# Diff attention: projections in three split terms, with their weights split when the stage begins and streamed in afterwards

## The reference

```
def _L1_attn_ref(x, W_attn, W_proj, lambda_q1, lambda_k1, lambda_q2, lambda_k2):
    B, T, E = x.shape                    # 4, 512, 512
    C = E // 2;  H = 16;  hd = E // H // 2;  scale = hd ** (-0.5)
    qkv = x @ W_attn                     # 512 x 1536
    q1, k1, q2, k2 = (qkv[..., n * C:(n + 1) * C].reshape(B, T, H, hd) for n in range(4))
    v = qkv[..., 4 * C:6 * C].reshape(B, T, H, 2 * hd)
    lam = jnp.exp(jnp.dot(lambda_q1, lambda_k1)) - jnp.exp(jnp.dot(lambda_q2, lambda_k2)) + LAMBDA_INIT
    attn1 = jnp.einsum('bthd,bshd->bhts', q1, k1) * scale
    attn2 = jnp.einsum('bthd,bshd->bhts', q2, k2) * scale
    score = jax.nn.softmax(attn1 - lam * attn2, axis=-1)
    out = jnp.einsum('bhts,bshd->bthd', score, v)
    return ((1.0 - LAMBDA_INIT) * out.reshape(B, T, E)) @ W_proj
...
x = x + _L1_attn_ref(_layernorm(x, axis=-1), ...)
```

## Time and profile before

| | us |
|---|---|
| median of 3 runs | 2392.21 (2390.53 to 2397.4) |
| the profiled execution | 2390.07 |
| its span, from the first to the last instruction | 2388.3 |
| PE busy | 2145.8 (90%) |
| DVE busy | 1730.0 (72%) |
| POOL busy | 1047.4 (44%) |
| ACT busy | 944.9 (40%) |

### The profile page before, as it was taken

One profiled execution on the slowest core, in us unless ns is written; L12 is line 12 of the kernel. 1 busy time (PEld: TensorE's weight loads), 2 busy tenths in 40 slices (PEclk: granted clock), 3 DMA queues, 4 the chain that ended last, 5 costly groups with the idle time before them and its releaser, 6 DMA issues. The chain is left out here.

```text
span 2388.3 us, 24939 instructions
## 1 busy us (share of the span) xinstructions
PE 2145.8 (90%) x7344; PEld 1102.4 (46%) x7344; DVE 1730.0 (72%) x2983; ACT 944.9 (40%) x1808; POOL 1047.4 (44%) x798
## 2 busy tenths in 40 slices
PE   4999999999999997897899998999789999999858
PEld 2555455555545552434555555464333434334234
DVE  2887788778788875886888988889455363655554
ACT  1442333334424433664656556465123232332321
POOL 2452453333425511233899898999411011110142
PEclk8999999999999998998999999999889999999879
DMA  7000000000000002466645535362322121221121
GB/s 265 19 23 19 19 18 23 18 22 23 14 23 19 23 23 86 166 232 237 220 149 195 179 109 213 115 222 82 118 76 75 46 75 53 71 71 49 49 110 53
DMA packets 95564, 214.87 MB, mean 90 GB/s; under 512 B 15832, under 2 KB 33112, under 8 KB 93032
## 3 DMA queue, kind: packets, MB, share of 16 engines
q1 hardware_dynamic: 77192, 156.18, 20.1%
q10 hardware_dynamic: 17760, 57.42, 6.7%
q0 software_dynamic: 512, 0.13, 0.0%
HBM read 146.30 MB, written 42.07 MB: 79 GB/s over the span
## 5 line engine op out<-in xcount | busy, mean ns | idle before, releaser
L1532 POOL TENSOR_TENSOR s_state<-s_b_rows,s_delta_u 128x1024 f32<-128x1024 f32 x128 | 303.5, 2386 | 37.0 <-DMA s_b_rows<-scan_bc 34.5
L1576 DVE TENSOR_TENSOR_SCAN s_state<-s_decay,s_state 128x512 f32<-128x512 f32 x256 | 305.0, 1212 | 15.5 <-ACT s_decay L1518 13.2
L834 POOL TENSOR_SCALAR a_prob<-a_prob,a_rsum 128x256 f32<-128x256 f32 x256 | 143.0, 577 | 385.8 <-DVE a_rsum L714 385.7
L1691 PE MATMUL c_bank<-c_xn_parts,c_w_parts 128*128 128x512 f32 (+1 forms) x1056 | 269.3, 405 | 6.5 <-DMA c_w_parts<-ffn_weights_lo 6.5
L1518 ACT ACTIVATE s_decay<-s_delta,s_a 128x512 f32<-128x512 f32 x256 | 173.5, 689 | 225.4 <-DVE s_state L1576 219.6
L384 DVE TENSOR_SCALAR f_picks<-f_mask,f_lut_xor,f_lut 128x260 int32<-128x260 int32 x512 | 225.9, 514 | 8.1 <-DVE f_mask L375 1.1
L1691 PEld LDWEIGHTS c_bank<-c_xn_parts,c_w_parts 128*128 128x128 f32 (+1 forms) x1056 | 195.9, 187 | 66.3 <-issue 20.7
L506 PE MATMUL a_bank<-a_xn_t,a_wq 128*128 128x512 f32 x512 | 224.3, 592 | 0.0
L567 PE MATMUL a_bank<-a_wo,a_out_t 128*128 128x512 f32 x512 | 222.3, 592 | 0.0
L2126 ACT ACTIVATE d_prob_t<-d_score 128x512 f32<-128x512 f32 x256 | 138.9, 595 | 194.5 <-PE d_score L2008 193.5
L394 DVE COPY_PREDICATED f_picks<-f_mask,f_picks 128x260 int32<-128x260 int32 x448 | 192.6, 489 | 20.8
(11 more groups left out here) (210 smaller groups left out, 3626.9 us busy)
## 6 DMA issues: line engine op xcount, KB each, us to landing
s_b_rows<-scan_bc SPq DMA_DIRECT2D x64, 512.0 KB, 3.7
c_w_parts<-ffn_weights_hi ACTq DMA_DIRECT2D x39, 512.0 KB, 3.6
c_w_parts<-ffn_weights_lo ACTq DMA_DIRECT2D x39, 512.0 KB, 4.6
f_idx<-in_idx SPq DMA_DIRECT2D x64, 130.0 KB, 2.1
ffn_weights<-f_picks SPq DMA_DIRECT2D x64, 130.0 KB, 1.8
d_qs<-d_hi SPq DMA_DIRECT2D x128, 64.0 KB, 2.0
d_ks<-d_hi SPq DMA_DIRECT2D x128, 64.0 KB, 2.0
d_factor<-in_factors SPq DMA_DIRECT2D x16, 512.0 KB, 3.6
```

The source lines that it names most:

```text
L1532: pool.tensor_tensor(self.state[:, s], row.broadcast_to([P, 2, T]), self.delta_u[:, h % 2], ALU.mult) \
L1576: dve.tensor_tensor_scan(self.state[:, s, e, :], self.decay[u % 2][:], self.state[:, s, e, :], 0.0, ALU.mult, ALU.add).then_inc(self.scann ...
L1691: mm = nc.tensor.matmul(banks[b][0:width[o], :], w_parts[:, n % SLOTS, w, at:at + width[o]], xn_parts[:, x_, k, :], start=((k, w, x_) == t ...
```

## The change

The q, k and v projections are done in three split terms of F32R instead of one F32 product: weights and normed features are each split into a rounded part and a rest, and a chain has 3 x 4 products (hi x hi, lo x hi, hi x lo).

- Features: ACT now rounds all four feature tiles (`xn_t[:, 0]`), and DVE subtracts to get the rest (`xn_t[:, 1]`); before, each of the two copied two tiles.
- Weights: SP loads them in 12 pieces of 256 KB into the memory of the probabilities. ACT rounds each piece, POOL subtracts to get the rest. The v parts stay in place (`wv`). The eight q and k units (512 KB each with both parts) are stored to a scratch in DRAM, from where SP loads them again for every pass, one unit of q and one of k per group (`load_unit`), into one buffer each.
- `load_unit` for the next group waits until PE has finished the projection that reads the buffer. In SP's order both loads stand ahead of the group's `stack`.
- The norm's tile now lies in the memory of `rsum` and `out_t`. The next sequence's norm is therefore applied in group 1, after `finish`, and no longer in group 0.
- The row of ones in `ks` is set in two steps, since units lie in a part of `ks` (and of `qs`) until they are stored.

```
+            def load_raw(m):
+                kind, n = PIECES[m]
+                if m >= SLOTS:
+                    sp.wait_ge(w_split, m - SLOTS + 1)
...
+                sp.dma_start(raw[:, m % SLOTS, :], source).then_inc(raw_in[m % SLOTS], 16)
+            def store_parts(m):
+                sp.wait_ge(w_split, m + 1)
+                sp.dma_start(scratch["diff_parts"][:, unit_of(*PIECES[m])], parts_of(PIECES[m]).bitcast(F32)) \
+                    .then_inc(w_stored, 16)
+            def load_unit(ring, in_pass, kind, after, g):
+                b, turn = ring.at((kind, after), in_pass)
+                sp.wait_ge(ring.full[b], turn)
+                m = "qk".index(kind)
+                sp.dma_start(unit[:, m].bitcast(F32), scratch["diff_parts"][:, unit_of(kind, g)]) \
+                    .then_inc(unit_in[m], 16)
...
             def one_pass(i, more):
                 for g in range(GROUPS):
                     if more or g + 2 < GROUPS:
-                        stack(ring, i, (g + 2) % GROUPS)
+                        pg = (g + 2) % GROUPS
+                        if more or g + 3 < GROUPS:
+                            for kind in "qk":
+                                load_unit(ring, i, kind, pg, (pg + 1) % GROUPS)
+                        stack(ring, i, pg)
...
             for g in range(2):
                 stack(first, 0, g)
+            for m, piece in enumerate(PIECES):
+                if piece[0] != "v":
+                    store_parts(m)
+            sp.wait_ge(w_stored, 16 * 2 * GROUPS)
+            for kind in "qk":
+                load_unit(first, 0, kind, 1, 2)
             load_factors(0, 0)
...
-            def project(ring, in_pass, kind, g):
+            def project(ring, in_pass, kind, g, parts):
                 b, turn = ring.at((kind, g), in_pass)
                 pe.wait_ge(ring.free[b], turn)
-                lo = "qk".index(kind) * D + g * P
-                for k in range(KD):
-                    mm = nc.tensor.matmul(banks[b][:], w[:, k, lo:lo + P], xn_t[:, k, :],
-                                          start=(k == 0), stop=(k == KD - 1))
+                for n, (wp_, xp) in enumerate(TERMS):
+                    for k in range(KD):
+                        w = parts[:, wp_, k * P:(k + 1) * P]
+                        mm = nc.tensor.matmul(banks[b][:], w, xn_t[:, xp, k, :], start=(n == 0 and k == 0),
+                                              stop=(n == len(TERMS) - 1 and k == KD - 1))
...
                         if st < 2 and proj_on:
-                            project(ring, i, "qk"[st], pg)
+                            pe.wait_ge(unit_in[st], (n + 1) * 16)
+                            project(ring, i, "qk"[st], pg, unit[:, st])
...
                     if g:
                         finish(n - 1, g - 1)
+                    if g == 1 and more:
+                        dve.wait_ge(acc_free, n + 1)
+                        norm_apply(nc, dve, norm, x, i + 1)
```

More of the change, by code:

```diff
@@ L175, with __init__ @@
 class Norm:
[L178 removed]
+    def __init__(self, core, sb, tag, xn=None):
         self.stats_done = core.sem(f"{tag}_ln_stats")
@@ L187, in __init__ @@
         self.rstd = sb(f"{tag}_rstd", [P, TT], F32)
-        self.xn = sb(f"{tag}_xn", [P, TT, D], F32)
+        if xn is None:
+            tile = sb(f"{tag}_xn", [P, TT, D], F32)
+            xn = [tile[:, tt, :] for tt in range(TT)]
+        self.xn = xn
 def start_at_one(eng, *sems):
@@ L242, in norm_ahead @@
     for tt in range(TT):
-        nc.vector.tensor_scalar(norm.xn[:, tt, :], x[:, i, tt, :], ahead.mean_var[:, tt, 0:1],
+        nc.vector.tensor_scalar(norm.xn[tt], x[:, i, tt, :], ahead.mean_var[:, tt, 0:1],
                                 ahead.rstd[:, tt:tt + 1], ALU.subtract, ALU.mult) \
@@ L268, in norm_tensor @@
             mm = nc.tensor.transpose(banks[b][:, tt * P:(tt + 1) * P],
-                                     norm.xn[:, tt, k * P:(k + 1) * P], ident[:])
+                                     norm.xn[tt][:, k * P:(k + 1) * P], ident[:])
         mm.then_inc(ring.full[b], 1)
@@ L1832, in stage_diff_attention @@
     VD = D // DH
-    w = sb("d_w", [P, KD, 3 * D], F32)
+    unit = sb("d_unit", [P, 2, 2, KD * P], F32R)
+    wv = sb("d_wv", [P, 2, KD, D], F32R)
     wp = sb("d_wp", [P, KD, D], F32)
@@ L1838, in stage_diff_attention @@
     coef = sb("d_coef", [P, 1], F32)
-    norm = Norm(core, sb, "d")
-    xn_t = sb("d_xn_t", [P, KD, T], F32)
+    xn_t = sb("d_xn_t", [P, 2, KD, T], F32R)
     hi = sb("d_hi", [P, 2, T], F32R)
@@ L1850, in stage_diff_attention, with parts_of, unit_of @@
     out_t = sb("d_out_t", [P, GROUPS, T], F32)
+    norm = Norm(core, sb, "d", xn=[rsum[:]] + [out_t[:, g, :] for g in range(1, GROUPS)])
+    PARTS_AT = {("q", 0): unit[:, 0], ("k", 0): unit[:, 1]}
+    for n, step in enumerate([("q", 1), ("k", 1), ("q", 2), ("k", 2), ("q", 3), ("k", 3)]):
+        rows, h = (qs, 2 * HG + 2 * n) if n < HG else (ks, 3 * HG + 2 * (n - HG))
+        PARTS_AT[step] = rows[:, h:h + 2, :]
+    PIECES = [(kind, g) for g in range(2) for kind in "qk"] + [("v", k) for k in range(KD)] \
+        + [(kind, g) for g in range(2, GROUPS) for kind in "qk"]
+    TERMS = ((0, 0), (1, 0), (0, 1))
+    raw = prob_t[:].rearrange("p s j t -> p (s j) t")
+    SLOTS = 2 * HG
+    def parts_of(piece):
+        return wv[:, :, piece[1], :] if piece[0] == "v" else PARTS_AT[piece]
+    def unit_of(kind, g):
+        return "qk".index(kind) * GROUPS + g
     PER_PASS = RANK // B
@@ L1889, in stage_diff_attention @@
                  + rows_steps(0, 0, ROWS) + [("neg", 0)])
-    w_in = core.sems("d_in_w", 4)
+    wp_in = core.sem("d_in_wp")
+    raw_in = core.sems("d_raw_in", SLOTS)
+    w_rounded = core.sem("d_w_rounded")
+    w_split = core.sem("d_w_split")
+    w_stored = core.sem("d_w_stored")
+    unit_in = core.sems("d_unit_in", 2)
+    xn_rounded = core.sem("d_xn_rounded")
     lam_in = core.sem("d_in_lam")
@@ L1911, in _ @@
         def _(sp):
[L1912 to L1917, removed]
+            def load_raw(m):
+                kind, n = PIECES[m]
+                if m >= SLOTS:
+                    sp.wait_ge(w_split, m - SLOTS + 1)
+                source = dram["d_w"][n * P:(n + 1) * P, 2 * D:3 * D] if kind == "v" else \
+                    dram["d_units"][:, unit_of(kind, n), :]
+                sp.dma_start(raw[:, m % SLOTS, :], source).then_inc(raw_in[m % SLOTS], 16)
[9 more added lines that the diff above has]
+                    .then_inc(unit_in[m], 16)
+            for m in range(4):
+                load_raw(m)
             for n, name in enumerate(("lq1", "lk1", "lq2", "lk2")):
@@ L1921, in _ @@
             sp.dma_start(rowsel[:], dram["rowsel"]).then_inc(lam_in, 16)
-            load_part(1)
-            load_part(2)
-            sp.dma_start(wp[:], dram["d_wp"].rearrange("(k p) o -> p k o", p=P)).then_inc(w_in[3], 16)
+            for m in range(4, SLOTS):
+                load_raw(m)
+            sp.dma_start(wp[:], dram["d_wp"].rearrange("(k p) o -> p k o", p=P)).then_inc(wp_in, 16)
+            for m in range(SLOTS, len(PIECES)):
+                load_raw(m)
             def stack(ring, in_pass, g):
@@ L1977, in values @@
                 pe.wait_ge(ring.free[b], turn)
-                for k in range(KD):
-                    mm = nc.tensor.matmul(banks[b][:], xn_t[:, k, tt * P:(tt + 1) * P],
-                                          w[:, k, 2 * D:3 * D], start=(k == 0), stop=(k == KD - 1))
+                for n, (wp_, xp) in enumerate(TERMS):
+                    for k in range(KD):
+                        mm = nc.tensor.matmul(banks[b][:], xn_t[:, xp, k, tt * P:(tt + 1) * P], wv[:, wp_, k, :],
+                                              start=(n == 0 and k == 0),
+                                              stop=(n == len(TERMS) - 1 and k == KD - 1))
                 mm.then_inc(ring.full[b], 1)
@@ L2075, in _ @@
             for g in range(2):
[L2076 to L2080, removed]
+                for kind in "qk":
+                    pe.wait_ge(w_split, PIECES.index((kind, g)) + 1)
+                    project(first, 0, kind, g, PARTS_AT[kind, g])
+            pe.wait_ge(w_split, PIECES.index(("v", KD - 1)) + 1)
+            pe.wait_ge(wp_in, 16)
             for tt in range(TT):
@@ L2094, in features, with round_pieces @@
             def features(ring, in_pass):
-                for k in (1, 3):
+                for k in range(KD):
                     b, turn = ring.at(("xn", k), in_pass)
                     act.wait_ge(ring.full[b], turn)
-                    nc.scalar.copy(xn_t[:, k, :], banks[b][:]).then_inc(ring.free[b], 1)
+                    nc.scalar.copy(xn_t[:, 0, k, :], banks[b][:]).then_inc(xn_rounded, 1)
+            def round_pieces(a, z):
+                for m in range(a, z):
+                    act.wait_ge(raw_in[m % SLOTS], (m // SLOTS + 1) * 16)
+                    hi_part = parts_of(PIECES[m])[:, 0, :]
```

(38 more changed lines are left out.)

11 lines of the change are left out of this document (8 added, 3 removed).

## The result

The changed kernel takes 2445.74 us, the median of 4 runs (2444.03 to 2448.91), against 2391.65 (4 runs) for the kernel before: a ratio of 1.0224, 95% interval 1.0207 to 1.024. It is slower by some 54 us; the forecast was 2444. The profiled execution took 2446.64, with a span of 2444.8. PE is busy for 2144.2 us in it, against 2145.8.

A forecast was written before the change was run, and what follows sets the result against it. PE was taken to bound the diff stage, busy 46.7 of 50 us. Group changes of +39.7 and a beginning of +12.1 gave +51.8 on 2390.07, 2441.9; with the median 2.1 higher, 2444 us, range 2419 to 2462.

The forecast's parts named there:

- The order of SP: In groups that stream units, all 24 copies are issued behind K; next S = K + 17.6, PE stands 6.3 us.
- S: Moment when PE opens a group with two score products, right after waiting for the stacked copies.
- K: Moment when k's projection ends on PE in a group.
- Rival 2: Faster: SP's copies, issued late, still arrive in time; 38 chains save 24.3, beginning costs +6.2; 2374 us, chance 0.05.
- The clock: PE's granted clock halves after each 6.3 us pause, costing 2.0 us per group that starts so, between 0 and 4.
- Rival 1: The clock stays at 1.00 through PE's pauses: -20 over ten groups, -2.6 in the first chain; 2421 us, chance 0.15.
- What PE gains: Projection chains of 12 F32R products take 2.96 against 3.60: 0.64 a chain, 30.7 us over 48 if all on path.
- The beginning: Start of the diff stage: stores follow SP's 48 copies, end at 1762.1; S of group 1 comes 12.1 us later.
- The sum: Over the diff stage: +39.7 behind the first S and +12.1 at its beginning, +51.8 us in all.
- The signs that were named: Profile signs: late q copies, 5 to 7 us waits in groups 1 to 3, chain 2.96, 9 us first-unit wait.
- the moved norm and the longer features lie in the pause: In group n = 1, the extra norm and feature work hides in PE's pause; group 33.0 against 28.6, +4.4.

The follow-up runs named there:

- interleaved order: Changed kernel with SP's load of k's unit moved behind q's twelve copies instead of ahead of them: 2384.1 us, 0.9946 of the kernel before.
- the wait put into the kernel before: Kernel before, with q's twelve copies in the loop also waiting for k's `lo`: 2485.23 us, 1.0376 of the kernel before.
- the fillers: Changed kernel with unused F32 products added on PE in each of its pauses: 2423.16 us, 1.0109 of the kernel before.

## Why the prediction was right, point by point

- *The order of SP.* Right in mechanism and size: S came 17.0 to 17.5 behind K ahead of the ten groups that wait, where 17.6 was said, and groups 1 and 2 lasted 32.9 and 33.2 where 33.0 was said. The interleaved order and the wait put into the kernel before show it from both sides. Rival 2, faster, needed an issue under some 0.36 us; the copies show 0.62 to 0.64, at 64 KB and at 32. The Trainium skill (DMA: Bandwidth & Descriptors, section Issuing engines are not separate DMA queues) says that the time to initiate a DMA is usually small relative to the DMA itself. These copies do not bear it out: 64 KB would take 0.17 us at the 387 GB/s of the earlier trace rows, and SP takes 0.62 to issue them.
- *The clock.* The mechanism was right, and 2.0 a pause, taken from one stall of the kernel before, was close: the fillers show 2.3 in the mean, between 1.5 and 2.9. S to K was forecast at 15.4 and took 15.85 in the mean, K to S at 17.6 and took 17.25; that the two nearly cancel is luck. Rival 1 (2421, no fall of the clock) falls; the kernel with fillers is close to it, at 1.0109 times the kernel before.
- *What PE gains.* The chain of 12 takes 2.95 to 3.06 at full clock (2.96 was said, against 3.60 in the earlier trace rows), and the four chains of v at the end of a pass take 5.89 and 5.78, two in each. In the changed kernel q's and k's gain only shortens S to K; where the copies are no longer waited for, group 2 falls to 25.3, 1.4 under its 26.8, and group 3 from 53.3 to 49.5.
- *The beginning.* Stores landed by the time that was said: SP issues the first unit load 58.3 behind the stage's first DMA (1766.79 - 1708.46); the forecast, 1762.1 - 1703.88, was 58.2. S of group 1 is 12.4 later against that DMA, 12.1 was said. What PE waits for on the way is another thing than the forecast had: it waits 3.65 for the first unit and not some 9, since it has already stood 6.29 for the negated row maxima, where it stood 2.98 in the kernel before:

```profile
1756.30 1.19 PE L2008 MATMUL d_score<-d_qs,d_ks 97*128 97x512 f32 x2 [2.98 <-DMA d_qs<-d_neg_t]
```

  Their copy took 5.2 from issue to landing, against 1.9 before, while the stores were under way. The unit comes later still, so that the sum is not touched.
- *The sum.* From S of group 1 to that of group 15 the changed kernel takes 39.4 more, 39.7 was said. With the 12.4 that is 51.8, the forecast's own sum. The two profiled spans are 56.5 apart; of the rest, 4.6 lies ahead of the stage, whose first DMA starts at 1708.46 instead of 1703.88. In the profiles here it starts anywhere from 1703.3 to 1709.8, so a median that is met within 2 us is in part luck. The signs that were named came out, some of them roughly, but for two: the wait for the unit, and PE's wait ahead of group 2, which was 4.60 and not 5 to 7.
- *What was sized too low.* That the moved norm and the longer features lie in the pause was right only because the pause was there. In the interleaved order group 1 lasts 29.1, not less than the 28.6 of before. In its timeline PE stands 1.81 us behind the transposes, until the ACT roundings and DVE subtractions of the four feature tiles are done, where it stood 0.71 before:

```profile
1798.21 2.97 PE L2030 MATMUL d_bank<-d_xn_t,d_unit 128*128 128x512 f32 x12
...
1808.35 3.04 PE L2030 MATMUL d_bank<-d_xn_t,d_unit 128*128 128x512 f32 x12 [0.18 <-DVE d_mx L2273]
...
1823.53 0.71 PE L2069 MATMUL d_score<-d_qs,d_ks 97*128 97x512 f32 x2
1826.06 0.73 PE L2069 MATMUL d_score<-d_qs,d_ks 97*128 97x512 f32 x2 [1.81 <-DVE d_xn_t L2245]
```

  The chains of q and k start 10.14 apart in this group and 9.50 apart in groups 2 and 3. In group 1 DVE applies the moved norm just ahead of the row maxima there, so it probably costs the other 0.6; no run leaves it out. Together that is 1.8 in each of three groups, and from S of group 1 to that of group 15 this kernel is 20.1 shorter than the kernel before, where rival 2 had 24.3.

## What to carry to other kernels

When loads are added to a queue that is written out by hand, look at what stands behind each added wait: here two loads whose data were harmless held 24 copies, because the second load waits for the later of two projections. Put each load directly ahead of the copy that has the later wait anyway. Count DMA issues by their number before counting bytes, and price every pause of PE with the slow clock behind it as well as with its own length.

## What the runs showed of the hardware

A copy of 32 KB takes about as long to issue on SP as one of 64 KB, 0.64 against 0.62 us. While ACT issued four stores of 512 KB, four of SP's issues took 1.1 each instead of 0.62; that the one caused the other was not tried apart. And added products that compute nothing took about 22 us off the program: the granted clock behind the ten waits was 1.00 with them, and 0.50 without.
